# A graph network on one core: the feature stage between two edge passes, written out in five batches with rooms of their own

## What is computed

```python
score = clip(einsum('ehd,ehd->eh', q[edge_dst], k[edge_src]) / sqrt(HD), -10, 10)
alpha = softmax of score over the edges of one destination
wv = segment_sum(alpha * v[edge_src], edge_dst)          # "first pass" over edges
y = wv @ Wp.T + bp
x = feat + y
h = _layernorm(x, ln_g, ln_b)
h = gelu(h @ W1.T + b1) @ W2.T + b2
return x + h                                             # then x1 = layernorm(feat + (x + h))
# second layer: proj_s = x1 @ W_s.T, proj_t = x1 @ W_t.T, attention over edges, agg @ W_fc.T
```

## Time and profile before

| | |
|---|---|
| time, median of 3 runs | 3197.64 us (3196.48 to 3199.67) |
| profiled execution, span | 3825.7 us, 55082 instructions |
| busy: TensorE, VectorE, GpSimd, ScalarE | 2265.8, 2190.3, 2033.0, 1162.1 us |
| first pass, in the profile | about 151 to 1525 us |
| feature stage, in the profile | about 1525 to 1871 us |

### The profile page before, as it was taken

The page is one execution under the profiler, slowest core; times in us unless marked ns, Lnnn a source line. Parts: engine busy times, 40 slices in busy tenths (PEclk is TensorE's granted clock), DMA queues, the critical chain, the costliest instruction groups (busy, mean ns, idle before and its releaser), DMA issues.

```text
span 3825.7 us, 55082 instructions
## 1 busy us (share of the span) xinstructions
PE 2265.8 (59%) x11461; PEld 1680.5 (44%) x11462; DVE 2190.3 (57%) x6388; ACT 1162.1 (30%) x2751; POOL 2033.0 (53%) x1970
## 2 busy tenths in 40 slices
PE   4566666666666666587534445444444446777777
PEld 2244444444454444475423323332322235565565
DVE  5466556565665666234245556555555576666766
ACT  0145545554554555243212212222222210111111
POOL 0255555555565554212366676767776635444443
PEclk9788878887888788798766666666666668889988
DMA  4666666666666664122477777777777765666665
GB/s 139 208 174 183 177 184 185 179 185 181 185 183 188 187 181 129 54 69 74 139 205 217 219 218 216 213 212 216 212 213 215 211 209 187 194 193 199 202 199 171
DMA packets 365776, 698.67 MB, mean 183 GB/s; under 512 B 77382, under 2 KB 247104, under 8 KB 365739
## 3 DMA queue, kind: packets, MB, share of 16 engines
q0 software_dynamic: 134784, 425.63, 38.2%
q1 hardware_dynamic: 220666, 256.40, 21.4%
q10 hardware_dynamic: 10288, 16.23, 1.2%
HBM read 597.23 MB, written 100.85 MB: 182 GB/s over the span
## 4 chain that ended last, share of the span: by engine, by line
PE 31%; another core or an unknown queue 23%; DVE 21%; issue 16%; DMA 3%; DVEq 2%; SPq 2%; ACT 1%; POOL 1%; ACTq 0%; POOLq 0%
PE ps_px L916 10%; DVE sb_score L1517 4%; PE ps_pa L929 3%; PE ps_px L929 3%; DVE sb_prod L1706 3%; PE ps_pn L1052 3%; PE ps_px L1014 2%; DVE sb_wide L1699 2%; PE ps_px L1023 2%; PE ps_pa L1093 2%; DVE sb_wide L1526 1%; PE ps_px L892 1%; DVE sb_prod L1511 1%; DVE sb_parts L1911 1%
## 5 line engine op out<-in xcount | busy, mean ns | idle before, releaser
L916 PE MATMUL ps_px<-sb_parts 128*128 x2430 | 457.1, 349 | 609.8 <-DVE sb_wide L1699 465.4
L916 PEld LDWEIGHTS ps_px<-sb_parts 128*128 128x128 bf16 x2430 | 276.8, 121 | 757.2 <-DVE sb_wide L1699 490.7
L793 POOL DMA_INDIRECT sb_ring<-proj_rows,sb_idx x324 | 360.5, 1113 | 281.8 <-issue 164.1
L793 POOL DMA_INDIRECT sb_ring<-kv_rows,sb_idx x324 | 320.4, 989 | 338.4 <-DVE sb_wide L1526 131.5
L929 PE MATMUL ps_pa<-sb_wide,sb_onehot 128*128 128x264 f32 x864 | 300.5, 480 | 260.4 <-DVE sb_wide L1526 201.3
L793 POOL DMA_INDIRECT sb_parts<-kv_rows,sb_idx x324 | 316.0, 975 | 204.0 <-DVE sb_wide L1526 102.1
L916 PE MATMUL ps_px<-sb_parts,sb_xwm 128*128 x2430 | 399.9, 310 | 31.6 <-issue 14.8
L793 POOL DMA_INDIRECT sb_w<-narrow_rows,sb_idx x324 | 348.7, 1076 | 101.0 <-issue 97.5
L929 PE MATMUL ps_px<-sb_wide,sb_onehot 128*128 128x264 f32 x756 | 257.9, 474 | 201.6 <-DVE sb_wide L1526 141.0
L1699 DVE TENSOR_TENSOR sb_wide<-ps_px,sb_ring 128x516 f32<-128x516 f32 x162 | 109.6, 687 | 431.1 <-remote 392.2
L916 PEld LDWEIGHTS ps_px<-sb_parts,sb_xwm 128*128 128x128 bf16 x2430 | 271.4, 112 | 163.9 <-issue 63.3
(11 more groups left out here) (265 smaller groups left out, 4535.1 us busy)
## 6 DMA issues: line engine op xcount, KB each, us to landing
sb_bits<-dst_short SPq DMA_DIRECT2D x280, 192.0 KB
x_edges<-sb_ring SPq DMA_DIRECT2D x54, 768.0 KB
sb_slots<-x_edges SPq DMA_DIRECT2D x54, 768.0 KB
x_edges<-sb_slots SPq DMA_DIRECT2D x27, 768.0 KB
sb_w<-x_edges SPq DMA_DIRECT2D x27, 768.0 KB
sb_msg<-lo_rows SPq DMA_DIRECT2D x28, 576.0 KB
kv_rows<-sb_slots ACTq DMA_DIRECT2D x25, 256.0 KB, 2.9
sb_parts<-part_rows SPq DMA_DIRECT2D x28, 193.5 KB
```

The costliest lines, as they stand in the source:

```text
L793: pool.indirect_dma_start(out=out[:, i, :], out_offset=None, in_=rows, in_offset=bass.IndirectOffsetOnAxis(ap=idx[:, 2 * p + i:2 * p + i + ...
L916: mm = pe.matmul(into, hots_t[L][:, 2 * p + i, :], flat(visit_parts[:, bass.ds(parity, 1), a, 0:width]), start=(a == 0), stop=(a == 2))
```

## The change

The loop over batches is written out on every engine, and the order inside is another. Each of the five batches has a room of its own for x and for y (`x_rooms`, `y_rooms`), laid into memory that the first pass leaves free: batch 0 in `wqkv` and `msg`, batches 1 and 2 in `ring` (the places of the gathers of pairs 0 to 5), batches 3 and 4 in `parts` (pairs 9 to 14). So the loads go to other places of the queues. x of batch 0 is loaded on SyncE when the q, k, v stage has done its last product; y of batch 0 on ScalarE's queue after the loop of the first pass, before the last visit; batches 1 and 2 on SyncE after message 5 of the last visit; batch 3 and x of batch 4 after the last message; y of batch 4 after the last store. `first_stored` and `most_stored` give how many visits must have been stored for that. GpSimd's twenty adds have no wait but for these loads. VectorE takes the first statistics of batch 0 in the middle of the last visit's finish, and those of the following batch ahead of the network's results; the first norm of the following batch goes between `xs` 2 and 3. TensorE transposes the following batch's h right behind the network, ahead of x1; `hT` has a room of its own; the projections use five banks of PSUM in place of four. The first norm has its own `stats0`, `mv0`, `rstd0`.

```diff
+            sp.wait_ge(xt_used, W + 1)
+            load_inputs(0)
             sp.wait_ge(tables, 2)
             sp.dma_start(y_rows[N_NODES:NP, :].unsqueeze(0),
...
                         with sp.Fori(0, total - 2) as u:
                             visit(sp.snap(u + 2), u)
+                        sp.wait_ge(slots_free[0], total * PAIRS + 6)
+                        sp.sem_inc(sp_seen, 1)
+                        sp.wait_ge(y_stored, most_stored(sp) * 16 + 1)
+                        sp.sem_inc(sp_seen, 1)
+                        for it in (1, 2):
+                            load_inputs(it)
+                            load_sums(it)
                         products_out(visit_before(sp))
+                        sp.wait_ge(slots_free[0], total * PAIRS + PAIRS)
+                        sp.sem_inc(sp_seen, 1)
+                        load_inputs(3)
+                        load_sums(3)
+                        load_inputs(4)
                         products_out(last_visit(sp))
...
-            load_inputs(0)
             second_parts, second_pass = edge_pass(1)
             sp.wait_ge(y_stored, total * 16 + 1)
             sp.sem_inc(sp_seen, 1)
-            load_sums(0)
+            load_sums(BATCHES - 1)
...
-            with pool.Fori(0, W // NB) as it:
-                pool.wait_ge(xw_in, it * 16 + 16)
+            for it in range(BATCHES):
+                rows, batch = x_rooms[it], y_rooms[it]
+                pool.wait_ge(xy_in[it], 32)
                 pool.sem_inc(pool_seen, 1)
-                pool.wait_ge(y_in, it * 16 + 16)
-                batch = y_batch
-
-                pool.sem_inc(pool_seen, 1)
-                pool.tensor_tensor(batch, batch, xw[:], ALU.add).then_inc(npl, 1)
+                pool.tensor_tensor(batch, batch, rows, ALU.add).then_inc(npl, 1)
...
+            pe.wait_ge(wp_act, total * 2 + 1)
+            h_transposed(0)
+            pe.wait_ge(ndot, 1)
+            for it in range(BATCHES):
+                mlp_in(it, 0)
                 for s in range(1, NB):
-                    mlp_in(s)
-                    mlp_out(s - 1)
-                mlp_out(NB - 1)
...
+                    mlp_in(it, s)
+                    mlp_out(it, s - 1)
+                mlp_out(it, NB - 1)
+                if it + 1 < BATCHES:
+                    h_transposed(it + 1)
+                x1_transposed(it)
+                projected(it)
...
             with act.Fori(0, total - 2) as u:
                 visits(act.snap(u + 1), u)
+            act.wait_ge(y_stored, first_stored(act) * 16 + 1)
+            act.sem_inc(act_seen, 1)
+            act.dma_start(y_rooms[0], y_rows[0:NB * P, :].rearrange("(w p) c -> p w c", p=P)).then_inc(xy_in[0], 16)
             visits(last_visit(act), visit_before(act), last=True)
             edge_onehots(last_visit(act), PAIRS - 1)
...
+                if more:
+                    first_roots(it + 1)
+                    for s in range(3):
+                        h_copied(it + 1, s)
+                act.wait_ge(nv, NVS["mv1", it, NB - 1] + 1)
                 act.activation(rstd[:, 0, :], mv[:, :, 1], ACT.Sqrt, bias=eps[:, 0:1]).then_inc(na, 1)
+                if more:
+                    for s in range(3, NB):
+                        h_copied(it + 1, s)
...
+            finish(last_visit(dve), "acc")
+            first_statistics(0)
+            for step in FINISH[1:]:
+                finish(last_visit(dve), step)
+            first_norm(0)
...
+            for it in range(BATCHES):
+                more = it + 1 < BATCHES
+                if more:
+                    first_statistics(it + 1)
+                dve.wait_ge(npl, NPS["xrb", it] + 1)
+                for s in range(3):
+                    sums_out_of(it, s)
+                if more:
+                    first_norm(it + 1)
+                for s in range(3, NB):
+                    sums_out_of(it, s)
```

More of the change, by code:

```diff
@@ L298, in build @@
         nd = sem("nd")
-        xw_in = sem("xw_in")
+        xy_in = [sem(f"xy_in{it}") for it in range(BATCHES)]
         nv = sem("nv")
@@ L507, in build @@
         GRAPH_ALL = 16 * len(GRAPH)
-        TABLES = {"blocks": 24, "linked": 54, "past": 56, "read": 57}
+        TABLES = {"blocks": 24, "linked": 53, "past": 55, "read": 56}
         @block.sync
@@ L1583, in _ @@
             visits(last_visit(dve), visit_before(dve), last=True)
-            for step in FINISH:
-                finish(last_visit(dve), step)
             dve.sem_inc(nv, 1)
@@ L1620, in batch @@
-            def batch(it, last=False):
-                dve.wait_ge(npl, it * NPL + NPS["xrb"] + 1)
-                for s in range(NB):
-                    dve.wait_ge(nt, it * NT + NTS[f"mlp{s}"])
-                    dve.tensor_tensor(xs[:, s], px[:, 4 + s % 2, 0:C], xw[:, s], ALU.add).then_inc(nv, 1)
-                statistics(it, [xs[:, s] for s in range(NB)], 1)
+                dve.wait_ge(nv, NVS["rs1", it] + 1)
+                if it == 0:
+                    dve.wait_ge(y_stored, total * 16 + 1)
+                    dve.sem_inc(dve_seen, 1)
@@ L1646, in batch @@
                 split(target, CW, (W // NB + it) * SPLITS + 1, W // NB + it)
-            first_norm(0)
-            with dve.Fori(0, W // NB - 1) as it:
-                batch(it)
-            batch(W // NB - 1, last=True)
-            dve.wait_ge(na, (W // NB) * NA)
+            dve.wait_ge(na, len(NA_ORDER))
             dve.sem_inc(t_ready, 1)
```

262 lines of the change are left out of this document (135 added, 127 removed).

## The result

The changed kernel takes 3144.12 us, median of 4 runs (3139.43 to 3147.71), beside 3197.98 us (3196.48 to 3199.67) for the kernel before on the same chip: ratio 0.983, 95% interval 0.9816 to 0.9844. That is 54 us faster; 40 were forecast, and 3144 lies in the range of 3130 to 3178.

A forecast was written before the change was run, and what follows sets the result against it. Bound taken: engines waiting on each other in the feature stage, 26.2 us between networks and the stretch from last visit to first network. 42 + 23.4 - 22.5 - 3 = 40 us off 3197.6 gives 3158 us; range 3130 to 3178.

The forecast's parts named there:

- Between batches: Gap between networks: 26.2 us falls to 15.7, saving 10.5 us four times, 42 us.
- The start without a collision: Last visit to first network, nothing colliding: network starts at 1542.6 in place of 1566.0, 23.4 us saved net.
- 4.6 of them lost again: First pass: its start 2.6 us later, and y's load delaying the last visit's gathers by 2 us.
- The collision: Last visit and finish: GpSimd's adds hold VectorE's clips, shift, denominators and norms, costing 22.5 us, plus 3 for messages.
- nothing held: Rival: VectorE slips between adds, or batch 0's adds fall behind the last clips; 65 us saved, 3132 us; chance 0.15.
- the clips alone held: Last visit: each clip waits for an add, a pair takes 3.04 us in place of 1.87; nine times, 10.5 us.
- 3 us for the messages: Last visit: cost taken for messages beside GpSimd's adds, between 0 (not held) and 10 us.
- 10 as the upper bound: Last visit: messages held like the norm, each taking its own add, 10 us more until the 16 adds are used up.
- messages held too: Rival: GpSimd's adds also hold the last visit's messages; collision 32.5 us, 33 us saved, 3165 us; chance 0.25.
- The clock: Rival: TensorE, nearly always busy in the feature stage, falls towards clock 0.81; 53 us more, 3210 us; chance 0.05.

The follow-up runs named there:

- before again: The kernel before, no edit, run for a second profile; it fell on chip A: 3825.97 us, one run.
- A: Label of a chip sort, not a run: the kernel before takes 3822 us there; the profile ahead of the prediction is of this sort.
- adds held: Changed kernel, GpSimd waiting behind its second add until batch 0's first norm is done: 3775.81 us (0.9878) on A; again, 3144.63 (0.9829) on B.
- B: Label of the other chip sort, not a run: the kernel before takes 3197.98, 3199 or 3202 us there.
- VectorE adds: Changed kernel with all 20 adds on VectorE in place of GpSimd, on B: 3141.52 us, ratio 0.9805.
- one early add: Changed kernel plus a tiny GpSimd add (128x1) between the last visit but one and the last visit's gathers, on B: 3171.48 us, ratio 0.9902.
- x late: Changed kernel, SyncE loading batch 0's x behind the first pass's zeros, rows, indices and node parts, on A: 3795.41 us, ratio 0.9915.
- late first batch: Changed kernel, batch 0's y loaded after the last products are stored, first statistics behind the denominators, on B: 3174.09 us, ratio 0.9916.
- serial: Changed kernel with the order between batches as before on every engine, only the loads early, on B: 3173.61 us, ratio 0.9926.

## Why the prediction came out right, and what in it was wrong

**Between batches.** 42 us forecast. The periods of before sum to 245.1 us in the profile ahead and 246.7 in before again, those of the changed kernel to 206.6: 38.5 to 40. The mechanism was right: the root is at 1340.81, the five norms pass in 1.71 us before the network's end at 1344.2. That the gap is 15.7 us to the tenth is luck in part: the projections start 6.1 us behind the network's end and not 6.8, and their 20 products take 9.6 to 9.7 us and not 8.9. The first period is 2 us longer than the others, as TensorE, idle for 11.4 us of waiting shortly before, starts it at a clock of 0.76 (last window above), between its two levels, and the first 64 products take 9.48 us, where those of the later networks take 7.31.

**The start without a collision.** I had 28.0 us gained, 4.6 of them lost again. On A the start fell from 43.9 to 16.3 with the adds held, 27.6; on B it is 16.4 and 17.1 where nothing collides (VectorE adds). The first gather is 2 to 6 us later; what y's load takes from the last visit's gathers no run tells.

**The collision.** This is the term that was mis-sized: 22.5 us, and 3 for the messages. On B it is 8 us (25.0 against 16.4 to 17.1), on A 34 (30.1 in the last visit, 3.7 behind it). Two errors lie in it.

One is where the adds fall. "GpSimd is done with its gathers at 1499.1", I wrote, 23 us ahead of the last message, and "I take them off the median as they are, unscaled". That distance is not a wait of engines in the feature stage but the tail of the first pass, and it belongs to an execution 628 us longer than the median. In the kernels profiled on B it is 11 us, and the start-up of 8.8 fills most of it, so that the first add (1228.51) just misses the last clip (1228.12). That is the second condition of my rival "nothing held" ("batch 0 falls behind the last clips", 3132 us), with a chance of 0.15 for the whole rival: the condition came true, its price did not, as the finish and the norms were held even so. That the change gained more than forecast is luck in this: clips and messages were spared by where the gathers happened to end. Where the adds meet them on B ("one early add") 30 us are gained and not 54. Two rows show how the passes differ. On A a gather waits for a message to free its place (GpSimd, before again); on B VectorE waits for gathers (the changed kernel):

```profile
1201.99 0.94 POOL L793 DMA_INDIRECT sb_ring<-kv_rows,sb_idx  x1 [5.16 <-DVE sb_wide L1526]
```
```profile
1223.44 0.69 DVE L1552 TENSOR_TENSOR sb_prod<-ps_px,sb_parts 128x512 f32<-128x512 f32 x1 [1.11 <-DMA sb_parts<-kv_rows,sb_idx]
```

They are typical of their passes (waits, the first pass; the total, how often, the longest):

```profile
POOL sb_ring L793 <- DVE sb_wide L1526: 135.9, 47, 7.6
```
```profile
DVE sb_prod L1552 <- DMA sb_ring<-kv_rows,sb_idx: 111.7, 104, 15.4
```

Over all places, GpSimd's gathers wait for messages for 312 us on A and 17 on B, VectorE waits for gathers for 237 us on B and 10 on A; for most of VectorE's waiting on A, 366 us, the profile names no engine. Where the gathers bound the pass, they end late, and little is left after them.

The other is the price once they meet. I had the clips alone held, so that a pair becomes 3.04 us, and took 3 us for the messages, 10 as the upper bound. Clip and message each take an add, a pair 6.4 us. (The reason given for a small price, that a message streams as many numbers as a norm, does not hold either: the rows have 128x512 for one and 128x256 for the other.) So on A it is the rival "messages held too": its collision was 32.5 us, the measured one is 34. Its 33 us saved are also what the trace shows up to the fifth network (1780.21 for 1810.87 in the rows ahead, 31); the kernel with x late saves 26 us of 3822 by the medians, 0.7%, or 0.85% by the ratio, the rest being within the scatter of the passes. The Trainium skill (SBUF — State Buffer, "Who interferes with whom") had it: two SBUF inputs, or `tensor_scalar` in a two-port mode, hold and are held for the whole instruction, `tensor_reduce` never. The rows agree in each kind: messages 2.5 to 3.2 us, clips 2.85, norms 9.2 for five, reductions 0.67, products from PSUM 0.68. I gave the rule 0.25.

**The sum** on B: 57.5 to 59 us from the last message to the fifth network (19.0 at the start, 38.5 to 40.1 over the periods), up to 1 lost from there to the first gather of the second pass (57.3 for 56.4), 2 to 4 at the pass's start: 52 to 57, measured 54. With passes that move by 5 us either way it could not be told more closely. It takes the 44.0 of the start from chip A; the late first batch, with 47.2 on B, speaks for it, and serial, with 61.4, for the periods, but the kernel before itself has no profile there. Of the forecast's own terms, 42 became 38.5 to 40, 28.0 became 27.6, the 4.6 lost became 2 to 4, and the 25.5 of the collision became 8: the last accounts for the difference between 40 and 54.

**The clock**, my slower rival: no fall. The second network runs at 1.00, the stretch behind it at 0.89, both mostly the upper level of 2.4 GHz, and the later periods stay at 51.1 us.

## What to carry to other kernels

Before taking any interval out of a profile, set its span against the measured median; where they differ, ask of each interval whether it is part of what differs, and do not carry over those that are. Work on an otherwise idle GpSimd is not free: list the clips, norms and two-input instructions of VectorE that will stand beside it, price each at one whole GpSimd instruction (here 2.9 us), and if VectorE itself has idle time, put the work there. Holding the work back only moves the collision, so look at what stands where it then falls due.

## What the runs showed of the hardware that I had not expected

- GpSimd's start-up between its last gather and its first add, 8.7 to 9.7 us in eight kernels, is paid once: a tiny add ahead of the last visit took the 7.3 us, and after 30 more gathers the next add began at once. In that idle time of the changed kernel the instruction queue (q14) moved two packets.
- In the meetings with adds of 2.88 us, an instruction of VectorE of 0.16 us takes as long as the add (a clip 2.85). The adds amid the last visit of "one early add" take 2.88 to 3.44 us, little more than alone; where four messages had begun first, the add was held (4.94).
- The same program's first pass ran at a clock of 0.80 to 0.82 on one chip, between its two levels, and 0.96 to 0.97 on the others, with 1345 and 1065 us from the first gather to the last (before again, and the changed kernel). GpSimd's busy time in it was nearly the same (796 and 818 us). Why the chips differ stays open.
